# Ten first columns in one register load, and the selection four tiles ahead, in the sum stage of a graph network kernel

## What is computed

```
def layer(h, params):
    W, b, g, beta = params
    h = h * norm_out
    agg = jax.ops.segment_sum(h[src], dst, num_segments=n)
    agg = agg * norm_in
    out = agg @ W + b
    out = _layer_norm(out, g, beta)
    out = jax.nn.gelu(out, approximate=False)
    return (out, None)
h, _ = jax.lax.scan(layer, features, (Ws, bs, ln_g, ln_b))
...
x = _layernorm(x + h, axis=-1)
```

## Time and profile before

| | us |
|---|---|
| median of 3 runs | 1680.89 |
| lowest and highest | 1677.46, 1686.68 |
| the profiled execution, its time | 1669.91 |
| the profiled execution, span from first to last instruction | 1668.2 |

### The profile page before, as it was taken

One profiled execution on the slowest core, in us unless ns is written; L12 is line 12 of the kernel. 1 busy time (PEld: TensorE's weight loads), 2 busy tenths in 40 slices (PEclk: granted clock), 3 DMA queues, 4 the chain that ended last, 5 costly groups with the idle time before them and its releaser, 6 DMA issues.

```text
span 1668.2 us, 29286 instructions
## 1 busy us (share of the span) xinstructions
PE 1110.4 (67%) x6235; PEld 916.9 (55%) x6235; DVE 880.2 (53%) x2153; ACT 528.1 (32%) x853; POOL 846.9 (51%) x1023
## 2 busy tenths in 40 slices
PE   7665378677596695776776696679956769992000
PEld 7444123666575575656656585667846667882000
DVE  6445577245354372463563274326733226776776
ACT  4132230232332332233333232333323333441444
POOL 1554300545445464455455365445745445765886
PEclk9556559788898897798898898789987889996555
DMA  0930000523514415225225324441244448545998
GB/s 14 377 130 3 2 1 6 159 82 126 158 57 139 133 69 170 78 107 163 71 106 164 107 76 138 139 126 66 91 139 147 149 126 321 189 169 180 312 302 291
DMA packets 98038, 224.52 MB, mean 135 GB/s; under 512 B 14496, under 2 KB 14496, under 8 KB 97968
## 3 DMA queue, kind: packets, MB, share of 16 engines
q0 software_dynamic: 34432, 104.72, 21.2%
q1 hardware_dynamic: 57200, 107.52, 17.9%
q10 hardware_dynamic: 6336, 11.54, 1.9%
HBM read 137.91 MB, written 85.82 MB: 134 GB/s over the span
## 4 chain that ended last, share of the span: by engine, by line
PE 53%; issue 12%; DMA 10%; DVE 8%; POOL 5%; ACT 4%; another core or an unknown queue 3%; ACTq 2%; DVEq 2%; POOLq 0%; SPq 0%
PE ps_a L1200 16%; PE ps_y L1220 9%; PE ps_y L1221 9%; PE ps_y L1225 9%; DMA rows<-h_rows,slot 4%; POOL rows L507 3%; DMA rows<-h_rows,idx_f 2%; PE ps_y L1216 2%; DMA h_rows<-rows 2%; PE ps_a L1115 2%; DVE agg_t L607 2%; PE ps_a L1181 1%; ACT agg_t L958 1%; DVEq L821 1%
## 5 line engine op out<-in xcount | busy, mean ns | idle before, releaser
L1200 PE MATMUL ps_a<-sel,rows 128*128 128x128 f32 x2560 | 407.0, 323 | 278.1 <-DVE sel L789 122.8
L1200 PEld LDWEIGHTS ps_a<-sel,rows 128*128 128x128 f32 x2560 | 377.1, 233 | 309.6 <-issue 309.0
L456 POOL DMA_INDIRECT rows<-h_rows,slot x290 | 279.8, 965 | 258.3 <-issue 124.6
L995 ACT ACTIVATE agg_t<-ps_a 128x508 f32 x320 | 190.7, 596 | 520.7 <-PE ps_a L1200 369.8
L464 POOL TENSOR_TENSOR s_lo<-agg_t,s_hi 128x512 fp32r<-128x512 f32 x168 | 216.9, 1293 | 251.3 <-ACT s_hi L1000 251.3
L789 DVE TENSOR_SCALAR sel<-iota,by_tile 128x128 f32<-128x128 f32 x344 | 126.0, 370 | 395.6 <-PE ps_a L1200 207.2
L1220 PE MATMUL ps_y<-w_hi,s_hi 128*128 128x512 f32 x672 | 268.5, 400 | 10.9 <-ACT s_hi L1000 10.8
L1221 PE MATMUL ps_y<-w_lo,s_hi 128*128 128x512 f32 x672 | 267.6, 398 | 0.0
L1225 PE MATMUL ps_y<-w_hi,s_lo 128*128 128x512 f32 x672 | 183.5, 396 | 0.0
L862 DVE BATCH_NORM_STATS2 small<-ps_y 128x6 f32<-128x512 f32 x168 | 117.3, 698 | 96.1 <-PE ps_y L1225 95.9
L1220 PEld LDWEIGHTS ps_y<-w_hi,s_hi 128*128 128x128 f32 x672 | 129.0, 192 | 42.0 <-issue 15.1
(11 more groups left out here) (210 smaller groups left out, 1268.2 us busy)
## 6 DMA issues: line engine op xcount, KB each, us to landing
h_rows<-rows SPq DMA_DIRECT2D x124, 256.0 KB, 2.0
h_rows<-agg_t SPq DMA_DIRECT2D x1, 20480.0 KB
out<-agg_t SPq DMA_DIRECT2D x78, 256.0 KB
agg_t<-in_x SPq DMA_DIRECT2D x19, 1024.0 KB, 5.7
h_rows<-rows ACTq DMA_DIRECT2D x44, 256.0 KB, 2.3
w_raw<-in_Ws SPq DMA_DIRECT2D x32, 256.0 KB
rows<-h_rows,slot POOLq DMA_INDIRECT x290
rows<-in_ln_g SPq DMA_DIRECT2D x8, 256.0 KB, 3.8
```

Source lines behind the costliest of these rows:

```text
L456: g.indirect_dma_start(out=rows[:, k, :], out_offset=None, in_=table[:, :], in_offset=bass.IndirectOffsetOnAxis(ap=slot[:, k:k + 1], axis=0))\
L995: a.activation(agg_t[:, :, bass.ds(r0 + 1, P - 1)], ps_a[k % GS][:, :, 1:P], ACT.Copy)\
L1200: m = mm(ps_a[k % GS][:, b, :], rows[:, k, b * P:(b + 1) * P], sel[:, k % GS, :], start=True, stop=True)
```

## The change

- Both VectorE and ScalarE load the first columns of a whole group at the head of the group's loop body, with one call over ten elements of `q0`, and no longer one value for each tile.
- AHEAD is 4. Selection n+4 is made behind the column addition of tile n, and so behind the eviction of tile n; VectorE's own wait for `agg_ok` is gone, since `ev_ok` comes later.
- At k = 4 and 9 the indices come behind that selection.

```
-AHEAD = 3
+AHEAD = 4
...
+        def first_columns(engine, t):
+
+            return nc.values_load_multi_w_load_instructions(q0[0:1, bass.ds(t, UN)], engines=(engine,),
+                                                            min_val=0, max_val=N + 1)[1]
...
                         t = group * UN
                         i = ib * UN + t
+                        firsts = first_columns(mybir.EngineType.DVE, t)
                         for k in range(UN):
-                            r0 = dve.value_load(q0[0:1, bass.ds(t + k, 1)], min_val=0, max_val=N + 1)
-                            dve.wait_ge(agg_ok, done(i + k + 1))
-                            select(t + k + AHEAD, k + AHEAD)
                             dve.wait_ge(edge_ok, done(i + k))
                             dve.sem_inc(dve_tick, 1)
                             dve.wait_ge(ev_ok, done(i + k + 1))
-                            col = agg_t[:, :, bass.ds(r0, 1)]
+                            col = agg_t[:, :, bass.ds(firsts[k], 1)]
                             v.tensor_tensor(col, ps_a[k % GS][:, :, 0:1], col, ALU.add).then_inc(edge_ok, 1)
+                            select(t + k + AHEAD, k + AHEAD)
                             if k % GS == GS - 1:
                                 indices(L, t + k // GS * GS + UN, k // GS)
...
                 with act.Fori(0, its) as group:
                     t = group * UN
+                    firsts = first_columns(mybir.EngineType.Activation, t)
                     for k in range(UN):
                         i = ib * UN + t
-                        r0 = act.value_load(q0[0:1, bass.ds(t + k, 1)], min_val=0, max_val=N + 1)
                         hold(agg_ok, done(i + k + 1))
                         hold(ev_ok, done(i + k))
-                        a.activation(agg_t[:, :, bass.ds(r0 + 1, P - 1)], ps_a[k % GS][:, :, 1:P], ACT.Copy)\
+                        a.activation(agg_t[:, :, bass.ds(firsts[k] + 1, P - 1)], ps_a[k % GS][:, :, 1:P], ACT.Copy)\
```

## The result

The kernel after takes 1719.15 us (median of four runs, 1717.59 to 1727.66), the kernel before beside it 1683.27 us. The ratio is 1.0227, with a 95% interval of 1.0181 to 1.0273: 2.3% slower, clear of no change though not of 2%. The profiled execution has a span of 1715.8 us, 47.6 more than before.

What follows compares the result with a forecast made beforehand. It took the sum stages to be a loop of latencies with no engine full, sums held while gathers run. Terms +13 + 0 + 12 - 48 = -23 us, on the median 1680.9 us, gave 1658 us; range 1605 to 1715.

Steps and rivals of the forecast that it cites:

- The other 16 heads: Group heads neither first in a layer nor at tile 20: load block hidden, 0 us; uncovered up to 3 us each.
- the hold: In sum stages, a finished sum is seen late while gathers are under way; release some 1.1 us after the last gather.
- the early start: If a half's last tile is seen in time, GpSimd starts the next gathers at once; 2.4 us saved where seen.
- The size of the block: Ten loads with register work at each group's head on VectorE: 4.4 us, between 3.1 and 5.8.
- What the lead brings: Second half of a group seen early, one in two of GpSimd's 39 waits: 20 x 2.4 = -48 us.
- Tile 20: Head at tile 20 of each of 8 layers, behind the bias: +1.6 us each, +13 us in all.
- The first group of a layer: Block hidden in VectorE's 9.54 us idle before its first selection; without that cover 4.4 us each.
- Selection before indices: At k = 4 and 9 the index copy stands behind a selection: 40 x 0.3 = +12 us.
- the block of loads: Rival, 0.20: ten registers loaded one after another, 5.8 us on VectorE, stop selection and eviction; 1710 us, 1737 at worst.
- The chain alone: Rival, 0.10: hold releases as before, lead brings nothing, block hidden but for tile 20; +25 us, 1706 us.
- The hold fed by the gathers: Rival, 0.20: early start joins two gather runs, time returns at next release; within 0.5% of 1681 us.
- GpSimd's wait for sums: Sign in the profile after: 80 to 100 us instead of 132.2; still 130 would mean the lead brought nothing.

Runs made afterwards that it cites:

- E15: The kernel after, unchanged, against the kernel before at 1517 us: ratio 1.0395.
- E2: The kernel before with only the blocks of ten loads added, its order and lead of three kept: 1584.6 us against 1521.0, ratio 1.0421.
- E10: After's order with a lead of five and single loads without computation and assertion, against the kernel before at 1680 us: 0.9948.
- E1: The kernel before with only after's order and lead of four, single loads kept: 1519.6 us against 1521.0, ratio 0.999.
- E13: After's order and lead of four alone, single loads kept, against the kernel before at 1517 us: ratio 1.0012.
- E17: After's order and lead of four alone, single loads kept, against the kernel before at 1519 us: ratio 0.9999.
- E11: The kernel after with two loads of five per group on both engines instead of one of ten, against the kernel before at 1680 us: 1.008.
- E4: The kernel before with single loads without computation and assertion on both engines, against the kernel before at 1521 us: ratio 0.991.
- E8: After's order and lead of four, with single loads without computation and assertion, against the kernel before at 1520 us: 0.9898.
- E12: The kernel before with single loads without computation and assertion on VectorE alone, against the kernel before at 1680 us: 0.9956.

## Why the prediction was wrong

It gave 1658 us with a range of 1605 to 1715; it was 1719.2. Step by step:

- **"The other 16 heads: 0 us, hidden by the hold" failed.** It set the block's end 5.7 us after the release and the fifth tile's sum at about 8, ahead of a release after 9.6. The term was put at nothing; tiles 10 to 19 took 57.1 us more and the later groups that are not a layer's last 10.8. Measured in layer 7: the block begins 1.5 us after the release, the column behind it comes at 7.1 us, and the fifth tile is evicted at 10.3 us. TensorE had stood for 5.28 us, and its next run took 7.73 us for 48 matmuls, 1.29 a tile, at a granted clock of 0.71. Both runs of gathers grew, by 1.5 us together. The step compared the block with the whole period of the loop; what has to cover it is TensorE's stock of selected tiles, four of 1.03 us each in E15, less VectorE's column and selection. Of the 57.1 us a part is not this step's but that of the early start (the fourth point), and the two were not separated on this chip; on a quicker one, where nothing is held, the blocks cost 27.7 us at the same tiles and 6.8 in the later groups.
- **The size of the block, 4.4 us, was right outside the hold.** E2 has a mean of 4.43 us on VectorE, as 3.8 to 4.4 or 5.1, since loads took 1.1 to 1.2 or 2.3 us; the register work is done for each value, as was assumed. In the kernel after the mean is 5.0 because of the hold (next point). By the rule of the Trainium skill ("Runtime: NRT & Kernel Launch", instruction fetch mechanics: about 200 ns for each register, in bulk too) the estimate for ten is 2.0 us. Here the registers are loaded from a table in SBUF. The trace is near it for the 13 groups of 32 whose load takes 2.3 us on VectorE, and not for the other 19, at 1.1 to 1.2.
- **A block inside the hold was not foreseen.** Where the early gathers join the run before, blocks took 7.6 to 10.9 us, above the upper bound of 5.8. The hold slows a sequencer's own instructions, as the longest of the register instructions (0.7 us) show, and a block has twenty of them in a row.
- **"What the lead brings: -48 us" was not realised as a saving.** The early start is there (6.3 us from run to run), but at most once in a layer and not at 20 places, and the three runs around it took 31.8 us instead of 27.9. Tiles 0 to 9 gained 29.3 us by it, and the held stretch behind took that back. The warning beside the term, that joined runs are held longest, was right and had been left out of the sum: E10, without a block, shows it too (30.2 us for the three). Where nothing blocks (E1, E13, E17) the lead is worth 0 within 0.3%.
- **Tile 20: +1.6 us was right in its sum.** Measured 1.9 in layer 1 and 13.8 over the eight layers, against +13. In layer 1 two deviations cancel, which was luck: the first column came 3.8 us behind the bias and not 4.4, and TensorE's run of six tiles took 8.4 us and not 7.7.
- **The first group of a layer: 0 was right** (3.1 us from first matmul to first column in both kernels).
- **Selection before indices: +12 us** was not measured by itself. On the quicker chips the whole order, with the lead, is at 0 (E1), so no such cost is left in the sum there.

Of the rivals, the block of loads (0.20, 1710 to 1737, "decides from about 5 us on") is what happened; its chance was too small, and its threshold too high. In E11 blocks of 2.5 us still cost 0.8%. The chain alone had nearly the same time (1706) by another cause, which E1 excludes on the quicker chips. The hold fed by the gathers (0.20) happened too, at the joined runs; it does not explain the loss alone, since E10, with it and without a block, is at 0.9948. In the list of what the profile would show, GpSimd's wait for sums at 110.3 us lay between the two marks of 80 to 100 and 130, and so told nothing: the wait had moved to the indices and to TensorE.

The best kernel that ran is E4: the order and single loads of before, without the assertion and its register work, at 0.991 where the kernel before takes 1521 us (E8 is level; E12, half of it, is at 0.9956 where it takes 1680). The values are then no longer asserted to lie within the rows' range.

## What to carry to other kernels

Gathering the small sequencer work of ten tiles in one place saves little of it and makes a gap in the engine's stream; ask what stock of ready work the consumer has in time (tiles selected ahead by time per tile) and not whether the period of the loop is longer than the gap. Spread loads are hidden best: one value a tile behind waits that end later cost less than ten at a head, even though ten load instructions stand for one. A lead is a cover for a gap: it was worth nothing where there was none, and 2% where there was. And a place that hides work in the prediction (here the hold) has to be looked at in the state that the change brings about: here the early gathers moved the block at tile 10 into a longer hold.

## What was not expected of the hardware

- **A load of ten values into registers takes 1.1 to 1.2 or 2.3 us on VectorE (1.0 or 2.2 on ScalarE), by where it starts.** On both engines the short ones are those that start at a multiple of 80 bytes in the table; those that start 40 bytes further take the double. The loads of five in E11 (duration in ns: least, median, most):

```profile
L314 DVEq TENSOR_LOAD <-q x64: 17/1182/1202, 296.4 to 1396.4; - x64
L314 ACTq TENSOR_LOAD <-q x64: 550/1114/1142, 297.2 to 1394.7; - x64
```

  Most starts are now 20, 40 or 60 bytes behind a multiple of 80, and those take the 1.1 to 1.2 us of the median; the short ones are again mostly at multiples of 80. Since all starts are multiples of 20 bytes, these runs do not show which alignment a short load needs; a padded table was not tried.
- **Ten per cent between chips.** The same kernel before takes 1517 to 1521 us on three chips and 1680 on another. The whole hold (in the earlier trace rows a sum of about 1320.0 is evicted at 1323.53) is missing in the profiles of the faster ones, and there the longest register instruction at the loads' line is 218 ns and not 714 (E15, VectorE):

```profile
L314 DVEq FUSED_REGOPS  x320: 183/183/218, 276.1 to 1277.0; - x160
```

The cause of the hold is not settled. It goes with the chip that a run came from, and the prediction built its largest term on it.
